# Overwritten bf16 products at the head of each quarter of a graph network's sparse passes: five, four and two of them

## What is computed

```
L0 (twice):  c = leaky_relu(segment_max(x[src] @ W_msg + ea32 @ W_edge, dst) + x @ W_root + b)
L1:          w = relu(ea17 @ W1.T + b1) @ W2.T + b2
             y = relu(x @ Ws.T + bs + segment_sum(w * x[src], dst) @ Wn.T + bn)
L2 (2 hops): h = segment_sum(norm * h[src], dst)
L3:          y = segment_sum((x * out_deg**-0.5)[src], dst) @ W * in_deg**-0.5 + b
after each:  x = layernorm(x + y)
```

## Time and profile before

| | |
|---|---|
| three runs | 4715.11, 4729.38 and 16627.88 us (median 4729.38) |
| the profiled execution | 4719.18 us |
| its span, first to last instruction | 4717.4 us |
| mean granted TensorE clock | 0.84 |
| PE busy | 3553.3 us, 75% |
| DVE busy | 2491.6 us, 53% |
| POOL busy | 2377.0 us, 50% |
| ACT busy | 931.0 us, 20% |

### The profile page before, as it was taken

One profiled execution on the slowest core, in us unless ns is written; L12 is line 12 of the kernel. 1 busy time (PEld: TensorE's weight loads), 2 busy tenths in 40 slices (PEclk: granted clock), 3 DMA queues, 4 the chain that ended last, 5 costly groups with the idle time before them and its releaser, 6 DMA issues.

```text
span 4717.4 us, 64689 instructions
## 1 busy us (share of the span) xinstructions
PE 3553.3 (75%) x23472; PEld 2745.1 (58%) x23472; DVE 2491.6 (53%) x6351; ACT 931.0 (20%) x2714; POOL 2377.0 (50%) x2520
## 2 busy tenths in 40 slices
PE   3776777677647777777776667677777779999999
PEld 2454555444534545544444445455555569999999
DVE  4555666666636666666665455555555553223211
ACT  0100000000112222222222233322323220011111
POOL 5566666666466666666664566665555530000000
PEclk7777777787768888888887778878888889999999
DMA  5323232323224343333332222233333338777776
GB/s 147 101 62 72 62 76 64 73 62 73 63 63 106 96 106 100 105 97 99 102 104 66 68 77 75 72 91 97 101 108 100 108 100 273 271 271 265 261 262 214
DMA packets 192376, 555.51 MB, mean 118 GB/s; under 512 B 77639, under 2 KB 83239, under 8 KB 172519
## 3 DMA queue, kind: packets, MB, share of 16 engines
q1 hardware_dynamic: 67132, 335.46, 22.2%
q0 software_dynamic: 80432, 124.45, 12.8%
q10 hardware_dynamic: 44538, 92.03, 5.3%
HBM read 455.48 MB, written 96.37 MB: 117 GB/s over the span
## 4 chain that ended last, share of the span: by engine, by line
PE 46%; another core or an unknown queue 23%; DVE 14%; issue 8%; ACT 5%; ACTq 2%; DMA 1%; DVEq 1%; SPq 0%
PE banks L1446 17%; PE banks L1215 7%; PE banks L1171 5%; DVE scan L2257 4%; PE banks L1243 4%; DVE hot_key L2288 3%; PE banks L1168 3%; PE banks L1355 3%; PE banks L1187 3%; DVE hot_src L2290 2%; DVE hot_lo L1916 1%; ACT adj L1676 1%; PE banks L1363 1%; DVE back L2262 1%
## 5 line engine op out<-in xcount | busy, mean ns | idle before, releaser
L928 POOL DMA_INDIRECT gath<-table,ids x2496 | 2366.6, 948 | 1469.2 <-issue 681.7
L1215 PE MATMUL banks<-back 128*96 128x104 f32 (+11 forms) x6000 | 789.9, 280 | 164.1 <-issue 117.6
L1215 PEld LDWEIGHTS banks<-back 128*96 128x96 f32 x6000 | 725.8, 192 | 243.1 <-issue 176.7
L2288 DVE TENSOR_SCALAR hot_key<-banks,key_t 128x392 bf16<-128x392 int16 x1600 | 659.5, 412 | 311.1 <-remote 285.6
L1243 PE MATMUL banks<-hot_key,hot_src 128*128 128x392 bf16 x1600 | 457.8, 372 | 474.7 <-ACT adj L1676 263.0
L1446 PE MATMUL banks<-r_parts,adj_in 128*128 128x288 bf16 x6543 | 810.0, 287 | 5.5 <-DMA adj_in<-adjacency 4.2
L1446 PEld LDWEIGHTS banks<-r_parts,adj_in 128*128 128x128 bf16 x6543 | 802.5, 143 | 8.2 <-issue 4.3
L2257 DVE TENSOR_TENSOR_SCAN scan<-keep_of,scan,banks 96x512 f32<-96x512 bf16 x414 | 526.3, 1271 | 431.0 <-remote 327.9
L1243 PEld LDWEIGHTS banks<-hot_key,hot_src 128*128 128x128 bf16 x1600 | 149.9, 108 | 794.8 <-issue 743.4
L1171 PE MATMUL banks<-ea_of,w_edge_of 128*96 128x512 f32 x832 | 547.6, 743 | 17.8 <-issue 17.0
L1675 ACT ACTIVATE adj<-banks 128x160 bf16<-128x160 f32 x800 | 242.1, 303 | 1107.0 <-remote 718.8
(11 more groups left out here) (177 smaller groups left out, 2375.2 us busy)
## 6 DMA issues: line engine op xcount, KB each, us to landing
adj_in<-adjacency SPq DMA_DIRECT2D x114, 1568.0 KB, 6.6
adjacency<-adj ACTq DMA_DIRECT2D x100, 464.0 KB
gath<-table,ids POOLq DMA_INDIRECT x2496
ea_of<-in_ea_t SPq DMA_DIRECT2D x78, 512.0 KB
keep_of<-keep_max_d SPq DMA_DIRECT2D x52, 768.0 KB
adjacency<-adj ACTq DMA_DIRECT2D x100, 320.0 KB
adj_in<-adjacency SPq DMA_DIRECT2D x33, 928.0 KB, 4.8
ahead_of<-adjacency SPq DMA_DIRECT2D x33, 640.0 KB
```

The costliest lines, as they stand in the source:

```text
L928: pool.indirect_dma_start(gath[:, b, t, :], None, tables[p][:, :], bass.IndirectOffsetOnAxis(ap=ids[:, 1, n:n + 1], axis=0),).then_inc(s_g ...
L1215: m = pe.matmul(band_ps[g % 2][:, at:at + n], rows_in[:, q % 2, t * D:(t + 1) * D], hot_dst[:, q % 2, t, first:first + n], start=False, st ...
L2288: ve.tensor_scalar(hot_key[:, h, a, :], key_places_ps, key_t[:, 0, a, bass.ds(n, 1)], None, ALU.is_equal)
```

## The change

`keep_running(to, n, times)` is new. It issues `times` bf16 matmuls of 128 rows, 96 columns of weights (`iota_b[:, 0:n]`) and 512 moving columns (`iota_b` four times over) into a PSUM bank, each with `start=True, stop=True`. What they leave is overwritten by the next product into the bank, which starts with `start=True`. They signal nothing.

In `turn` there are five of them per quarter in pass 0 and four in pass 1, into `turn_ps[q % 2]`. The wait on `s_scan` moves from behind the waits on `s_ea` and `s_gath` to ahead of the five or four products, since they write into the bank that the scan frees; the other two waits stay ahead of the transposes. In `hidden` there are two per quarter, into `hid1_ps`, behind all of its waits.

```diff
@@ -1156,14 +1156,20 @@
+                def keep_running(to, n, times):
+
+                    for _ in range(times):
+                        pe.matmul(to, iota_b[:, 0:n], iota_b[:, :].unsqueeze(1).to_broadcast([P, QT, P]), start=True, stop=True)
+
                 def turn(p, q):
 
                     i, k, base = quarter_of(p, q)
+                    if p > 0 or q >= 2:
+                        pe.wait_ge(s_scan, base + q - 1)
+                    keep_running(turn_ps[q % 2], D, 5 if p == 0 else 4)
                     if k == 0:
                         pe.wait_ge(s_ea[i % 2], 16 * pair_loaded(p, i))
                     pe.wait_ge(s_gath[k], 16 * QT * (PAIRS * p + i + 1))
-                    if p > 0 or q >= 2:
-                        pe.wait_ge(s_scan, base + q - 1)
                     for t in range(QT):
@@ -1352,6 +1358,7 @@
                     else:
                         pe.wait_ge(s_copied[2], BANDS)
+                    keep_running(hid1_ps, D, 2)
                     pe.matmul(hid1_ps, weights(2), columns, start=True, stop=True).then_inc(s_hid_ps, 1)
```

## The result

| | before | after |
|---|---|---|
| median of six runs | 4723.28 us | 4754.41 us (4747.83 to 4761.66) |
| the profiled execution | 4719.18 us | 4754.76 us |
| its span | 4717.4 us | 4753.0 us |
| mean granted clock | 0.84 | 0.899 |
| PE busy | 3553.3 us, 75% | 3869.5 us, 81% |

The ratio is 1.0067, with a 95% interval of 1.0056 to 1.0077. The change costs 31 us. That is less than the 2% that counts here as a difference, and the interval still leaves no doubt about its sign. The forecast was 4765 us. (One of the six runs before is the 16627.88 us of the table further up; the median stands without it.)

What follows compares the result with a forecast made beforehand. The prediction took POOL's gathers and PE's late signals, not PE's speed, as the bound. 4719 + 0 + 28 + 10 = 4757 us profiled; the median is 10 us above, 4767, rounded to 4765; range 4430 to 4980.

Steps and rivals of the forecast that it cites:

- The bound: Passes 0 and 1: POOL's gathers, 4.99 us a quarter, plus 2.0 us idle per eight for late PE signals, not PE's speed.
- the first rival: Passes: PE at full clock signals in time, POOL loses its idle 2.0 us; 4550 us, 4089 at the most; 28%.
- The products' price: On PE: 218 ns each at full clock, 499 us of PE time in all, 998 us if the clock stayed low.
- Passes 0 and 1: Products fit in PE's idle time within each cycle of eight gathers: 0 us if the clock rises, 408 us without cover.
- Pass 2: Two products a quarter in pass 2: 31% of 91 us charged, 28 us, bounds 0 and 91.
- The 31%: Share of added PE time paid in pass 2, where 660 products ahead took the pace from 6.15 to 6.38 us.
- The tails: Some seven quarters at each pass's end, DVE and PE busy, no cover for the products: 10 us, at most 17.
- The clock: Passes 0 to 2: a higher PE clock returns 0 us, since full-clock cycles are no shorter; 665 if PE were the bound.
- the 68 to 70: Sign in the passes: 68 to 70 POOL gathers in 100 us if right; above 72 or below 66 the step fails.
- The rival by which the clock pays: Passes: PE held at full clock signals promptly and shortens the gather cycles; 4550 us, to 4400; 28%.
- The rival of the delayed signal: Products ahead of PE's turn delay its signal to POOL, so each is paid in the cycle: 250 us, 4970; 25%.
- The rival of the clock that stays: Passes: PE's pauses remain, the clock stays low, products cost 318 and 288 ns in passes 0 and 1; 4860 us; 7%.

## Why the prediction was right, point by point

**The bound.** The prediction put the pace of passes 0 and 1 on POOL: 4.99 us of gathers a quarter, and 2.0 us after every eighth for a signal of PE that comes late whatever PE's speed. The trace after bears it out: the cycles of eight gathers last 11.7 to 11.8 us at the median, whatever the clock, as before. POOL's pauses in the trace before end, at the median, 5.5 us (pass 0) and 5.1 us (pass 1) after PE has finished the product whose signal POOL lacks. Two details need a correction. Not every cycle has eight gathers (155 of 196 in the two passes do). And fast PE and prompt signals are not seen together only without gathers: pass 0 with three times the products has both. The chips of the prompt kind bear out the gathers' share from another side: without late signals the same kernel runs at 5.0 us a quarter and is over in 4045 us. That is a little under the floor of 4089 us that the first rival named, and it was a chip without late signals that reached it, not a clock.

**The products' price.** Estimated at 218 ns; measured 216 ns, back to back at full clock.

**Passes 0 and 1: 0 us charged, 18.7 us paid** (from first to last gather, 12.4 in pass 0 and 6.3 in pass 1; the 14.9 and 11.6 us above have the seams in them). This is the term that was too small. The step held that a cycle of eight gathers does not grow while PE has idle time in it. It grows little, by 0.07 and 0.09 us at the median, 3 and 5% of the products' time in it, but over the 104 pairs of quarters of each pass that would be about 17 us (an estimate from the medians). Beside that, POOL pauses more often, 27 times more in the two passes. The step expected that a turn later by up to 1.09 us would not reach POOL, since POOL is late itself. That it does now and then reach it fits the rows, but no run shows by itself whether the turn's delay, or the moved wait, is what does it.

**Pass 2: 28 us charged, 8.9 paid** (from first to last gather). The term was too large by a factor of three. The 31% came from the 660 products run ahead in the second half of the pass, and in those same rows the second half of the pass did not slow at all with two products more a quarter, 376 gathers in 600 us before and after. The 31% was not a price of two products more a quarter; what else slows that half was not looked into.

**The tails: 10 us charged.** POOL's wait at the seams grew from 30.59 to 33.42 us and, between passes 1 and 2, from 38.15 to 43.55, 8 us together. These rows of its timeline are of before and of after:

```profile
1283.71 0.94 POOL L928 DMA_INDIRECT gath<-table,ids  x1 [30.59 <-DMA table<-y]
2551.45 0.94 POOL L928 DMA_INDIRECT gath<-table,ids  x1 [38.15 <-DMA table<-node]
```

```profile
1299.09 0.94 POOL L928 DMA_INDIRECT gath<-table,ids  x1 [33.42 <-DMA table<-y]
2578.55 0.94 POOL L928 DMA_INDIRECT gath<-table,ids  x1 [43.55 <-DMA table<-node]
```

This term was about right. The dense stage and the rest moved by -0.2 us. The total was 38 us charged and 35.6 paid (18.7 + 8.9 + 8.2 - 0.2), so the good agreement is in part luck: two errors of opposite sign, 19 us too little and 19 us too much.

**The clock: 0 us.** This step carried the forecast. The clock did not come near 1.00 as foretold but to 0.90 and 0.91; for 0.99 in pass 0 it took three times the products. POOL's gathers in 100 us are 67.3 and 67.6, a little under the 68 to 70 that were to show the step right and above the 66 at which it was to fail. The rival by which the clock pays gave 4550 us, and it fell: from 0.84 to 0.90 the time went up by 0.7% on the first chip, and from 0.83 to 0.89, 0.93 and 0.96 by 1.0, 2.5 and 3.8% on the second. The Trainium skill (TensorE: Matmul & The Clock Gate, Part 1) says that activity releases the throttle. With that the trace agrees, and matmuls are faster at the mean: one of line 1171 (line 1177 after) took 743 ns before and 655 ns after. What does not follow is a gain for the kernel, for PE's matmuls did not set its pace.

**The rival of the delayed signal** was wrong in its size: it gave 250 us, half of 499, and the rows have 31 to 47 us for the first 499, and 63 to 75 for each further 499. Its mechanism may still be what the 18.7 us are made of, as said above. The rival of the clock that stays fell with the rise to 0.90.

## What to carry to other kernels

Before an engine is given work to lift its clock, compare whole cycles of the loop at both clocks in the trace: if they last as long at 1.00 as at 0.70, the clock has nothing to return, and the added work can cost something even where it fits in idle time. Its price depends on the cover. With POOL as a steady bound the products of one pass cost 0 to 0.1% of the kernel here. With pauses in the loop the first set of all cost 0.7 to 1%, which is 6 to 9% of the added work's own duration. Without the gathers it was 42% of that duration. And look at what ends the waits of the engine that does set the pace, since that, not the busiest engine, is where the time is.

## What the runs showed of the hardware

**The same kernel takes 4043 to 4048 us on some chips and 4723 to 4767 us on others**, a difference of some 17% that dwarfs the change, at spreads of 0.3% on each. Four chips were of the first kind and two of the second. In the slower ones PE's signals reach DVE and ACT some 2.5 to 5 us after the matmul's end in the rows shown (707.71 - 705.17 us above, and the earlier trace rows), 3.2 us at the median for ACT's copies in the kernel before, and the profile puts most such waits down to "remote". The ends of matmuls are modelled, so the rows do not tell a late signal from a matmul that really ended later. In the quicker ones they come at once, 0.04 us at the median for the same copies: in the run with the moved wait alone PE ends the product at 718.85 us, and the scan starts at 718.95:

```profile
716.93 1.92 PE L1177 MATMUL banks<-ea_of,w_edge_of 128*96 128x512 f32 x2
...
718.95 1.27 DVE L2264 TENSOR_TENSOR_SCAN scan<-keep_of,scan,banks 96x512 f32<-96x512 bf16 x1 [2.76 <-PE banks L1177]
```

Shown is that without gathers the signals are prompt on a chip of the late kind too, that they are prompt there beside gathers when PE is busy for 98% of the time, and that gathers do not delay them on the prompt kind. Not shown is whether the gathers' issue alone does it there, or the chain of waits around the gathers, or PE's own idle time, and what differs between the chips: the three kernels with gathers that nobody reads all ran on prompt ones. That the kinds are a property of the chips is itself argued only from the fact that all runs of one chip agreed.

**Gathers are dear through POOL, not through their traffic.** 128 rows cost POOL 1.25 us; with the rows loaded by SP in plain DMAs the kernel takes 3316 us on a chip where it took 4767, and on prompt chips gathers beside that into a spare buffer left pass 0 at its pace. That is no version to use, since plain loads don't gather; it is the size of what the gathers hold up, 4767 - 3316 = 1450 us on a late chip and, if the kernel without gathers takes the same there, some 730 on a prompt one.
